# Attention row maxima from a key difference with three score banks, and the output's scaling on GpSimd

## The reference

```python
x = x + attention(layernorm(x), Wq, Wkv, Wout, bout)      # 16 heads of 64
x = x + feed_forward(layernorm(x), U1, V1, b1, U2, V2, b2)  # rank 32, width 512

def attention(x, ...):
    q, k, v = split_heads(x @ Wq, x @ Wkv)                # rotary on the first 32 of 64
    q, k = rope(q), rope(k)
    sim = einsum('bhid,bhjd->bhij', q, k) * 64 ** -0.5    # 1024 x 1024 for each head
    out = einsum('bhij,bhjd->bhid', softmax(sim), v)
    return merge_heads(out) @ Wout + bout
```

## Time and profile before

| | |
|---|---|
| median of 3 runs | 1557.01 us (1556.73 to 1557.29) |
| the profiled execution | 1557.27 us |
| its span, first to last instruction | 1555.5 us |
| mean granted TensorE clock | 0.986 of full speed |
| TensorE (PE) busy, share of the span | 1424.9 us, 92% |
| VectorE (DVE) | 1222.0 us, 79% |
| GpSimd (POOL) | 977.8 us, 63% |
| ScalarE (ACT) | 778.3 us, 50% |

### The profile page before, as it was taken

The page is one execution under the profiler, slowest core; times in us unless marked ns, Lnnn a source line. Parts: engine busy times, 40 slices in busy tenths (PEclk is TensorE's granted clock), DMA queues, the critical chain, the costliest instruction groups (busy, mean ns, idle before and its releaser), DMA issues.

```text
span 1555.5 us, 25971 instructions
## 1 busy us (share of the span) xinstructions
PE 1424.9 (92%) x7289; PEld 546.8 (35%) x7289; DVE 1222.0 (79%) x1297; ACT 778.3 (50%) x1512; POOL 977.8 (63%) x501
## 2 busy tenths in 40 slices
PE   3689999999999999999999999999999999998886
PEld 1224333333333333333333333333333333333323
DVE  7787888788788878878788888878887887888744
ACT  3244554545454545555455454545545554544464
POOL 4388766658475665838476574848566584757731
PEclk9799999999999999999999999999999999999999
DMA  5312131221303121120313122031312204031002
GB/s 158 73 26 60 25 76 26 50 54 26 83 14 75 34 57 38 44 65 14 75 34 74 22 54 54 14 79 30 75 21 54 54 20 89 14 75 33 3 15 68
DMA packets 70209, 76.00 MB, mean 49 GB/s; under 512 B 27204, under 2 KB 36936, under 8 KB 69928
## 3 DMA queue, kind: packets, MB, share of 16 engines
q1 hardware_dynamic: 68736, 74.69, 21.4%
q10 hardware_dynamic: 1448, 1.00, 0.3%
HBM read 22.56 MB, written 2.36 MB: 16 GB/s over the span
## 4 chain that ended last, share of the span: by engine, by line
PE 56%; DVE 13%; issue 13%; POOL 7%; DMA 5%; ACT 3%; SPq 2%; DVEq 0%; ACTq 0%; POOLq 0%
PE O L388 18%; PE S L376 10%; PE S L377 8%; PE M L397 8%; DVE MX L603 5%; PE TILE L312 5%; DVE SUM L613 4%; DMA QK<-STAGE 4%; POOL SA L676 3%; PE TILE L322 2%; POOL STAGE L663 2%; ACT PF L515 2%; SPq L708 1%; PE TILE L306 1%; PE TILE L330 1%
## 5 line engine op out<-in xcount | busy, mean ns | idle before, releaser
L676 POOL TENSOR_TENSOR SA<-PF 128x1024 f32<-128x1024 f32 x256 | 616.5, 2424 | 372.5 <-DVE SUM L610 279.9
L515 ACT ACTIVATE PF<-S 128x512 f32<-128x512 f32 x1024 | 547.8, 599 | 564.9 <-PE S L377 564.1
L603 DVE TENSOR_REDUCE MX<-M 128x1 f32<-128x1024 f32 x504 | 614.5, 1219 | 229.3 <-PE M L397 229.1
L388 PE MATMUL O<-PF,V 128*64 128x512 f32 x2048 | 497.4, 607 | 0.0
L376 PE MATMUL S<-QK 128*128 128x512 f16 x1024 | 393.1, 384 | 0.0
L377 PE MATMUL S<-QK 128*128 128x512 f16 x1024 | 390.1, 381 | 0.0
L397 PE MATMUL M<-QK 64*128 64x512 f16 x1008 | 221.9, 437 | 65.9 <-DVE MX L603 47.7
L613 DVE TENSOR_TENSOR SUM<-SUM,SA 128x1024 f32<-128x1024 f32 x128 | 248.3, 1939 | 3.6 <-POOL SA L676 3.4
L397 PEld LDWEIGHTS M<-QK 64*128 64x128 f16 x1008 | 72.6, 140 | 370.8 <-DVE MX L603 247.9
L388 PEld LDWEIGHTS O<-PF,V 128*64 128x64 f32 x2048 | 124.5, 136 | 206.4 <-issue 149.8
L376 PEld LDWEIGHTS S<-QK 128*128 128x128 f16 x1024 | 99.9, 98 | 165.3 <-issue 64.2
(11 more groups left out here) (96 smaller groups left out, 749.0 us busy)
## 6 DMA issues: line engine op xcount, KB each, us to landing
QK<-STAGE SPq DMA_DIRECT2D x128, 256.0 KB, 3.9
QK<-STAGE SPq DMA_DIRECT2D x128, 128.0 KB, 3.1
RB<-den SPq DMA_DIRECT2D x128, 128.0 KB, 3.0
X<-in_L_attn_queries SPq DMA_DIRECT2D x4, 512.0 KB, 12.8
RT<-DS SPq DMA_DIRECT2D x128, 2.0 KB, 1.7
out<-X SPq DMA_DIRECT2D x8, 256.0 KB, 2.3
WRAW<-in_L_attn_Wkv SPq DMA_DIRECT2D x1, 1024.0 KB, 8.7
ROPE<-in_rope SPq DMA_DIRECT2D x1, 1024.0 KB, 12.0
```

Of the source, the lines that this page charges most:

```text
L388: mm = e.matmul(O[DH * z:DH * z + DH, :], V[:, h, kt * DH:(kt + 1) * DH], PF[:, t % SLOTS, z * HALF:(z + 1) * HALF], start=(kt == 0), stop ...
L515: e.activation(PF[:, t % SLOTS, z * HALF:(z + 1) * HALF], S[:, t % 2, z * HALF:(z + 1) * HALF], ACT.Exp, scale=EXP_SCALE).then_inc(exped, 1)
L603: e.tensor_reduce(MX[:, place % 2, q:q + 1], bank, AX, ALU.max).then_inc(max_read, 1)
L676: e.tensor_tensor(SA[:, (t // 2) % 2, :], PF[:, t % SLOTS, :], PF[:, t % SLOTS + 1, :], ALU.add).then_inc(two_summed, 1)
```

## The change

- **Keys' difference.** A new tensor KD holds, for each head, the high part of keys 0 to 511 minus the high part of keys 512 to 1023. GpSimd makes it from STAGE (`pool_keys_less`, at step 9), and the hand-over copies it: two more transfers for a head, so six.
- **Maxima.** A unit's two matmuls now give the difference MD (q times KD) and the second half's scores MR (q times k of 512 to 1023). ScalarE writes the positive part of MD to LEFT in SBUF (`act_left`), ahead of the exponentials in even steps and behind everything in odd ones. VectorE adds LEFT and MR and keeps the maximum in one instruction over 512 elements. MD has one bank, MR and LEFT have two: a unit waits until the last one's MD was read by ScalarE and the last but one was reduced.
- **Score banks.** S has three banks where it had four. Even steps use 0 and 1, odd steps 2 and 0. The waits on exponentials follow the bank.
- **Output copy.** `act_copy_out` moves behind the two exponentials of the step with kt == 2.
- **Multiplication by the inverse sums** moves from VectorE to GpSimd, at steps 13 and 26 (it was 16 and 26); after the loop it stays on VectorE.
- **Order of tiles.** k comes before q. The q and k tiles move from steps 1, 3, 5, 7, 9, 11, 13, 15 to 1, 3, 4, 7, 8, 10, 11, 13, and two V tiles from 8 and 10 to 14 and 16. In the last group the tiles of the feed-forward block's first product move from 12, 14, 16, 18, 21, 23 to 12, 18, 21, 22, 23, 24.
- Some small weights (V1, B1R, U1) now lie in SA until they are split, to make room.

```diff
-HAND = 4 * 16
+LOWEST = -3.0e38
+HAND = 6 * 16
...
+ORDER = "kq"
+QK_TILES = [(w, c, t) for w in ORDER for c in range(2) for t in ("rot", "pass")]
-QK_AT = (1, 3, 5, 7, 9, 11, 13, 15)
-V_AT = {8: (1, 0), 10: (1, 1), 22: (0, 0), 24: (0, 1)}
+QK_AT = (1, 3, 4, 7, 8, 10, 11, 13)
+KD_AT = 9
+V_AT = {14: (1, 0), 16: (1, 1), 22: (0, 0), 24: (0, 1)}
-NORM_AT = {16: 1, 26: 0}
+NORM_AT = {13: 1, 26: 0}
-DOWN_AT = (12, 14, 16, 18, 21, 23)
+DOWN_AT = (12, 18, 21, 22, 23, 24)
...
-        S = pb("S", [P, 2, N], F32)
-        M = pb("M", [P, N], F32)
+        S = pb("S", [P, 3, HALF], F32)
+        MD = pb("MD", [P, 512], F32)
+        MR = [pb(f"MR{n}", [P, 512], F32) for n in range(2)]
...
+        def bank_of(t, z):
+            return ((0, 1), (2, 0))[t % 2][z]
...
-                wait(e, exped, 2 * n + z - 3)
-                e.matmul(S[:, t % 2, rows], KHL[:, h, keys], QHH[:, h, rows], start=True, stop=False)
+                wait(e, exped, 2 * n - ((0, 2), (3, 1))[t % 2][z])
+                e.matmul(S[:, bank_of(t, z), :], KHL[:, h, keys], QHH[:, h, rows], start=True, stop=False)
...
+        def pe_unit(e, u, place, q, side):
+            wait(e, left_over, u)
+            wait(e, max_read, u - 1)
+            e.matmul(MD[:, :], QHH[0:DH, place, q:N:KT], KD[:, place, :], start=True, stop=True)
+            e.matmul(MR[side][:, :], QHH[DH:P, place, q:N:KT], KMH[DH:P, place, 512:N],
+                     start=True, stop=True).then_inc(unit_made, 1)
...
-            e.wait_ge(max_read, it.step(u))
-            pe_unit(e, it.step(u), place, q, M[:, :])
+            pe_unit(e, it.step(u), place, q, u % 2)
...
+        def act_left(e, u, side):
+            e.wait_ge(unit_made, u + 1)
+            wait(e, max_read, u - 1)
+            e.activation(LEFT[:, side, :], MD[:, :], ACT.Relu).then_inc(left_over, 1)
 
         def act_step(e, it, t):
...
-            if kt == 2 and (not it.first or h > 0):
-                act_copy_out(e, it.i * GH + h - 1, (h - 1) % GH)
+            more = not (it.last and t + LEAD >= STEPS)
+            if t % 2 == 0 and more:
+                act_left(e, it.step(t + LEAD), t % 2)
             for z in range(2):
...
+            if kt == 2 and (not it.first or h > 0):
+                act_copy_out(e, it.i * GH + h - 1, (h - 1) % GH)
             act_tiles(e, it, t)
+            if t % 2 == 1 and more:
+                act_left(e, it.step(t + LEAD), t % 2)
...
-            e.wait_ge(unit_made, u + 1)
             if q == 0:
                 wait(e, max_found, head - 1)
-            e.tensor_reduce(MX[:, place % 2, q:q + 1], bank, AX, ALU.max).then_inc(max_read, 1)
+            e.wait_ge(left_over, u + 1)
+            e.sem_inc(max_begun, 1)
+            e.tensor_tensor_reduce(LEFT[:, side, :], MR[side][:, :], LEFT[:, side, :], 1.0, LOWEST, ALU.add, ALU.max,
+                                   MX[:, place % 2, q:q + 1]).then_inc(max_read, 1)
...
-            if t in NORM_AT and not (it.first and NORM_AT[t]):
-                dve_norm(e, it.pair(NORM_AT[t]), NORM_AT[t])
...
+        def pool_keys_less(e, g):
+            e.wait_ge(rot_hi, g * 4 + 2)
+            e.wait_ge(pass_hi, g * 4 + 2)
+            keys = HIGH["k"]
+            e.tensor_tensor(KDS[:, :, :], keys[:, :, 0:512], keys[:, :, 512:N], ALU.subtract).then_inc(keys_less, 4)
...
+            if t == KD_AT and not it.last:
+                pool_keys_less(e, it.i + 1)
             if t % 2 == 0 and (not it.first or t > 0):
...
+            if t in NORM_AT and not (it.first and NORM_AT[t]):
+                norm(e, it.pair(NORM_AT[t]), NORM_AT[t])
...
                 sp.dma_start(QK[top, h, 0:3:2, :], STAGE[rows, 1:3, t, :]).then_inc(handed[h], 16)
+                sp.dma_start(KD[top, h, :], KDS[rows, t, :]).then_inc(handed[h], 16)
                 sp.dma_start(QK[low, h, 0:4, :], STAGE[rows, 0:4, t, :]).then_inc(handed[h], 16)
...
             for u in range(LEAD):
...
-                wait(pe, max_read, u - 2)
-                pe_unit(pe, u, u // KT, u % KT, (M[:, :], S[:, 0, :], S[:, 1, :])[u % 3])
-            pe.wait_ge(max_read, LEAD)
+                pe_unit(pe, u, u // KT, u % KT, u % 2)
```

More of the change, by code:

```diff
@@ L171, in build @@
         QT = QK[:, 3, :, :].rearrange("p a b -> p (a b)").bitcast(F32)
-        S = pb("S", [P, 2, N], F32)
-        M = pb("M", [P, N], F32)
+        S = pb("S", [P, 3, HALF], F32)
+        MD = pb("MD", [P, 512], F32)
+        MR = [pb(f"MR{n}", [P, 512], F32) for n in range(2)]
         O = pb("O", [P, HALF], F32)
         T = pb("TILE", [P, 512], F32)
-        HB = [S[:, side, z * 512:(z + 1) * 512] for side in range(2) for z in range(2)]
-        OB = [O[:, :], M[:, 0:512]]
-        TB = [T[:, :], M[:, 512:1024]]
+        HB = [S[:, 0, :], S[:, 1, :], S[:, 2, :], MR[0][:, :]]
+        OB = [O[:, :], MR[1][:, :]]
+        TB = [T[:, :], MD[:, :]]
         x_in = [sem(f"x_in{b}") for b in range(B)]
@@ L191, in build @@
         pass_hi, pass_lo, v_made = sem("pass_hi"), sem("pass_lo"), sem("v_made")
-        added = sem("added")
+        added, keys_less = sem("added"), sem("keys_less")
         handed = [sem(f"handed{h}") for h in range(GH)]
-        unit_made, max_read, max_found, max_row = (sem(n) for n in ("unit_made", "max_read", "max_found", "max_row"))
+        unit_made, left_over, max_begun, max_read, max_found, max_row = (sem(n) for n in ("unit_made", "left_over", "max_begun", "max_read", "max_found", "max_row"))
         scored, exped, pv_done, o_copied = sem("scored"), sem("exped"), sem("pv_done"), sem("o_copied")
@@ L374, in pe_scores @@
                 rows = slice(z * HALF, (z + 1) * HALF)
-                wait(e, exped, 2 * n + z - 3)
-                e.matmul(S[:, t % 2, rows], KHL[:, h, keys], QHH[:, h, rows], start=True, stop=False)
-                e.matmul(S[:, t % 2, rows], KMH[:, h, keys], QML[:, h, rows],
+                wait(e, exped, 2 * n - ((0, 2), (3, 1))[t % 2][z])
+                e.matmul(S[:, bank_of(t, z), :], KHL[:, h, keys], QHH[:, h, rows], start=True, stop=False)
+                e.matmul(S[:, bank_of(t, z), :], KMH[:, h, keys], QML[:, h, rows],
                          start=False, stop=True).then_inc(scored, 1)
@@ L391, in pe_values @@
             mm.then_inc(pv_done, 1)
-        def pe_unit(e, u, place, q, bank):
-            for c in range(2):
-                rows, keys = slice(DH * c, DH * c + DH), slice(c * 512, (c + 1) * 512)
-                mm = e.matmul(bank[:, keys], QHH[rows, place, q:N:KT], (KHL, KMH)[c][rows, place, keys],
-                              start=True, stop=True)
-            mm.then_inc(unit_made, 1)
+        def pe_unit(e, u, place, q, side):
[4 more added lines that the diff above has]
+                     start=True, stop=True).then_inc(unit_made, 1)
         def pe_next_unit(e, it, u):
@@ L429, in act_tile @@
                 e.wait_ge(tile_made, made)
-                if w == "q" and c == 0:
+                if w == ORDER[0] and c == 0:
                     for h in range(GH):
@@ L807, in _ @@
                     rot_low(pool, args, 0)
+                    if args[0] == "k" and args[1] == 1:
+                        pool_keys_less(pool, 0)
             ln_rstd(pool, 1)
@@ L862, in _ @@
             act.wait_ge(b1_turned, 1)
-            act.activation(B1[:, :], M[:, 0:FF // P], ACT.Copy).then_inc(b1_copied, 1)
-            act_max(act, 0, 0)
+            act.activation(B1[:, :], MR[0][:, 0:FF // P], ACT.Copy).then_inc(b1_copied, 1)
+            for u in range(LEAD):
+                act_left(act, u, u % 2)
+                if u == KT + 1:
+                    act_max(act, 0, 0)
             def body(e, it):
```

39 lines of the change are left out of this document (22 added, 17 removed).

## The result

The changed kernel took **1573.68 us** (median of 4 runs, 1571.04 to 1577.23) against 1556.91 before: 1.0109 times as long, with a 95% interval of 1.0088 to 1.0130. I had forecast 1547 and a range of 1514 to 1574, with faster the likeliest. The direction was wrong; the median lies just inside the range.

The account below looks back on a forecast made before the run. TensorE, busy 86 of a group's 90 us, was taken as the bound, so only its waits could be gained. 14 x 1.0 + 1.5 - 3.8 - 2 = 10 us less than 1557 gave 1547, range 1514 to 1574.

Parts of the forecast that it names:

- What the change removes: TensorE's waits in a group: stalls on maxima, OS and the hand-over go, within 4.8 us a group to win.
- The slack of one unit covers it: Units needing only the last but one reduced: over 2 us of slack, so even a 1.25 us reduction costs nothing.
- GpSimd's queue: From step 8: last low part done after 28.3 us, hand-over landing at 35.7, wanted at 36.8 at step 20.
- Rival B: GpSimd becomes the bound in steps 8 to 16, hand-over waited for at step 20: 21 us more, 1578; chance 0.22.
- The order on ScalarE: ScalarE's in-order queue: relus and the moved output copy make TensorE wait at several places, 3.8 us a group.
- Tile 11: Steps 10 and 11, one T bank: pass copy behind the output copy, stall 1.95 us for the 0.36 before.
- the values of step 28: Steps 26 and 27 have no tile; values of the next head wait for the output copy: stall 0.7 us.
- steps 2 to 4: The output copy pushes the odd relu to 5.37, so the unit waits: 0.25 us.
- the sum of new stalls: TensorE's new waits in a group: 0.8 + 1.95 + 0.7 + 0.25 + 0.1 = 3.8 us, against 4.8 gained.
- the bank 0 stall at step 0: Odd step's second-half scores wait for an exponential: 0.16 us at steps 0, 2, 12, 18, 26, together 0.8.
- The ends: Outside the middle groups: 3.8 us longer before the loop, 1.5 gained in the first group, about 2 lost in the last.
- Rival C: Whole kernel: new stalls equal the old, 0.7 us more a group than summed, 1554 to 1560; chance 0.14.

Follow-up runs that it names:

- experiment 7: Changed kernel with four banks for the scores and one for the second half's maxima MR: 1639.98 us, 1.0533.
- experiment 9: Changed kernel with a second, unused pass over MR on VectorE ahead of each maximum: 1600.41 us, 1.0277.
- experiment 4: Changed kernel with q and k tiles at steps 1, 3, 4, 7, 8, 11, 13, 15: 1598.99 us, 1.0272.
- Experiment 8: Changed kernel with groups 1 to 4 written out ahead of the loop, which then holds 10 groups: 1567.11 us, 1.0054.
- experiment 2: Changed kernel with the relu of step 0 moved behind that step's exponentials: 1567.65 us, 1.0068.
- experiment 6: experiment 5 with the V tile of step 24 at step 27, a first-group transposition tile moved, and the relu first at kt == 3: 1528.76 us, 0.9810.
- experiment 3: Changed kernel with the multiplication OS back on VectorE, at steps 16 and 26: 1568.36 us, 1.0069.
- experiment 1: Changed kernel with ScalarE's tile copies ahead of the output copy in the step with kt == 2: 1552.53 us, 0.9964.
- experiment 5: Changed kernel with the edits of experiment 1, experiment 2 and experiment 3 together: 1544.38 us, 0.9915.
- experiment 10: experiment 6 with the first q or k tile at step 0 instead of step 1: 1526.47 us, 0.9800.
- experiment 11: Kernel before the change, with only the multiplication OS on GpSimd, at steps 13 and 26: 1551.80 us, 0.9965.

## Why the prediction was wrong, point by point

- **What the change removes: right.** I had 2.8 us of waits on MX, 0.8 on OS and 0.6 on the hand-over going, and all of them went. (The text has 16 groups in the loop; it has 14, as the sum takes it.) "The slack of one unit covers it" was right too, and stronger than I put it (experiments 7 and 9).
- **GpSimd's queue: right, the figure in part by luck.** Its last low part was to be done 28.3 us after step 8 begins, with the hand-over in time by a narrow margin. It ended at 661.56, 28.1 us after, and in experiment 4 three microseconds more were too much. But the low parts took 1.16 us where the mean of the earlier trace rows had made me take 1.53, as in

```profile
658.08 2.37 POOL L704 TENSOR_TENSOR SA<-PF 128x1024 f32<-128x1024 f32 x1 [1.33 <-DVE SUM L633]
660.40 1.16 POOL L684 TENSOR_TENSOR STAGE<-YR,STAGE 128x512 f16<-128x512 f32 x1
```

and one sum on the way took 3.35 for 2.34, so that the two errors cancelled. Rival B, GpSimd as the bound, gives the right sign but is not what happened in the loop: no wait on the hand-over and none behind YR. At the two ends it did happen. GpSimd's sums took 2.48 us each, where the table of groups before had 2.42, although VectorE ran 512 more passes with one operand in SBUF beside them. The Trainium skill, SBUF — State Buffer, "Who interferes with whom", has such passes free of contention with GpSimd; the trace agrees to within these 2%.
- **The order on ScalarE: right as far as it went.** Tile 11 by 1.95 (measured 1.8), the values of step 28 by 0.7 (0.7), steps 2 to 4 by 0.25 (0.38 at the values and the unit behind them).
- **The step that failed is the sum of new stalls, 3.8 us a group; it is 4.9.** Two terms were missing. One is the turn of the loop on ScalarE: the bank 0 stall at step 0 was put at 0.16 us with four like it, where it is 0.98 (the four others are 0.07 to 0.15). I took ScalarE's idle time ahead of step 0 as free, and the first instruction there starts 1 us late. Experiment 8 shows it by leaving the turn out; in experiment 2 the gap is as long with another instruction in front. The other is VectorE's queue: the pass tile of step 3 stands behind a maximum that waits for the relu, 0.3 us at tile 4, which experiment 6 took away. At step 13 the order is the same, and tile 14 takes 0.2 us longer; no run took that away, but with VectorE's passes doubled (experiment 9) it grew. In a middle group a gain of 1.0 us became a loss of 0.3. Over the 14 groups the loss without spells is 2.9 us, since the last stretch, which ends in the last group, is 1.1 us shorter than before: 14 + 2.9 = 17 us from the forecast.
- **The ends were mis-sized**: 4.3 us net in the sum, about 13.8 measured in the profiled pair. The start of the units was near (4.3 us later at the thirteenth, where I had 3.8), and it was all won back by step 20 of the first group. Behind that OS on GpSimd costs 4.5 us in the first group and 1.6 in the last (experiment 3), where I had a gain of 1.5 and a loss of 2, the loss for OS in the last group alone. The rest, 3.2 us in the first group and 4.7 behind the last group's step 20, is open.
- **The clock was not in it.** The mean granted clock is 0.975 for 0.986 before; with the lower level at half of the upper, that is 2 x 0.025 x 1575 = 79 us at the lower level for 2 x 0.014 x 1555 = 44. In the loop a spell costs 1.6 us. The two there began 1.6 us and 1.3 us after the end of the 1.74 us wait at tile 11, in 2 groups of 14; with that wait at 0.55 us (experiment 1) there were none.

Together 17 + 9.5 + 3 = 29.5 us against 1577.2 - 1547 = 30 for the profiled run, which is 3.5 us above the median. Rival C, "0.7 us more a group than my sum", names what came in the loop, with 1.3; the time lies nearer to B's 1578, but GpSimd as the bound of the loop is not how it came about.

## What to carry to other kernels

When an in-order engine gets new work, put the new item into the queue at its place and follow each of its neighbours to the engine that waits for it; the busy share (here 68% on ScalarE and 58% on VectorE) says nothing about it, and most of the change's worth (from 1.1% slower to 1.9% faster) lay in such places. Idle time at the turn of a loop is not free time: measure the gap between the last instruction of one pass and the first of the next, and keep work out of it. And a second buffer between two engines can be worth more than a shorter pass: with 899 us of work on VectorE and one bank for MR the kernel was 5.3% slower than before, with 1215 us and two banks 2.8%.

## What was not expected of the hardware

ScalarE took 2.5 to 2.6 us between its last instruction in one pass of the loop and the first in the next, with either kind of instruction in front, and 1.5 us (just its data's arrival) where the groups were written out. The Trainium skill, Advanced Engine Details and Errata, "Control Flow Timing", has 108 ns for a compare-and-branch; by that alone a turn would be hardly visible, so the measured 1 us beyond the data's arrival has another cause that no run here names. In the loop its exponential also followed the relu 0.1 us later than in the written-out groups. The granted clock fell for single spells inside the loop in the kernels where TensorE waited some 1.7 us in each group (1.66 to 1.78), 0.6 to 1.6 us after the end of such a wait and in some groups alone; the kernel before and experiments 1, 5, 6, 10 and 11, with no wait over 1.19 us there, had none. Such a spell cost 1.6 us. That the wait is the cause was tried by experiment 1 alone.
